# Stage 1 written out step by step, the real spectra of w first, GpSimd's fold of v without its wait for the selection

## The chip, the cores and the metric

The kernel runs on one core of one Trainium2 chip. The metric is the device time of one execution in microseconds (us). TensorE multiplies matrices into PSUM banks, VectorE and ScalarE work on SBUF and PSUM, GpSimd on SBUF, and SyncE only issues DMA transfers. Each engine runs its own instruction list in order; they wait for each other by semaphores.

## The reference

`x` and `ctx` are 8 x 512 x 2048. The first half of the reference is an autocorrelation attention, the second an expert layer with a dense base (2048 x 2048) on every row:

```
q = layernorm(x);  k = v = ctx                       # sequence length L = 512, per channel
corr = ifft(fft(q) * conj(fft(k))).real
w, idx = top_k(corr, 12);  w = softmax(w)
out = sum_i w_i * v[min(idx_i + pos, L - 1)]         # clamped shift
x = x + tanh(g_xattn) * out
x = x + tanh(g_ffn) * ffn(layernorm(x))              # base matmul, gates, 8 experts of rank 16
```

## The kernel before, in words

Stage 1 computes the attention for 8 sequences x 4 chunks of 512 channels: 32 steps (`STEPS`), a step being one chunk of one sequence. All spectra are matrix products with cosine and sine tables. Inputs are mirrored and folded into sums and differences of halves first, so that the tables are 128 x 128. Stage 2 (`tensor_dense` and the like) is not touched by the change.

For chunk i the work is:
- SyncE loads v, x and the chunk for the statistics (`load_v`, `load_x`, `load_stats`) and stores results (`store`).
- GpSimd folds v (`fold_v`, L871 and L872; `join_v`, L877 and L879), adds the products of q and k (`sum_qk`, L884), folds q (`fold_q`, L860 to L864) and adds the products of w and v (`sum_wv`, six times L897).
- TensorE: `v_spectra`, `q_spectra` (L414), `correlate` (L465), and for the chunk before `turn_w` (transposes, L427), `w_spectra` (L446 with the upper part of w, L452 with the lower), `out_tiles` (L482).
- VectorE: `q_times_k` (L680 to L688), `w_low` (L695), `w_times_v` (L708 to L719 with the spectra of the first half of w, L726 to L734 with the second), `largest` (L752 to L768), `select` (four L777, then the reciprocal L781). L777 keeps the weights of the twelve largest: it reads `corr` and `halves`, both in SBUF, and adds them up. Every fourth step it also computes the layer norm's scales for the next sequence (`variance`, `scales`), whose last operation signals `ln1_ready`.
- ScalarE: `copy_w` (L552), `normalise` (L529), `take_stats` (L586 to L593), `copy_odd` (L559), `copy_v`, `exponentials`, `keep_out` (L579), `scale_w` (L572).

The steps overlap: in step i the engines correlate chunk i, fold and transform v of chunk i + 1, and transform w of chunk i - 1. TensorE's order in step i is `turn_w(i-1)`, `w_spectra(i-1)`, `correlate(i)`, `v_spectra(i+1)`, `out_tiles(i-1, 1)`, `q_spectra(i+1)`, `out_tiles(i-1, 0)`. VectorE's is `q_times_k(i)`, `w_low(i-1)`, `w_times_v(i-1)`, `largest(i)`, `select(i)`. GpSimd's is `fold_v(i+1)`, `join_v(i+1)`, `sum_qk(i)`, `fold_q(i+1)`, `sum_wv(i-1)`. ScalarE's is `copy_w(i-1)`, `normalise(i+1)`, `take_stats(i+5)`, `copy_odd(i)`, `copy_v(i+1, False)`, `exponentials(i)`, `copy_v(i+1, True)`, `keep_out(i-1, 1)`, `scale_w(i)`, `keep_out(i-1, 0)`.

Eight PSUM banks are used in two groups of four, `mine` and `other`, which swap each step. `v_spectra` writes its imaginary parts (L398) into banks that `w_times_v` reads until L734.

Steps 2 to 25 are a hardware loop of six turns with four steps each (L265); the others are written out. SyncE's list is written out in full.

Two waits of GpSimd ahead of `fold_v` matter here: for `w_made`, which counts the L777 of the step before, and, in steps 3, 7, ... 27, for `ln1_ready`.

```
if least(i) >= 1 and most(i) + 1 < STEPS:
    pool.wait_ge(w_made, 4 * i)
    if phase == NCH - 1 and most(i) + NCH < STEPS:
        pool.wait_ge(ln1_ready, i // NCH + 2)
    fold_v(i + 1)
```

Of the kernel before, what the change touches and what calls it, by code (L numbers as in the profile page):

```python
# [111 lines left out]
def flamingo_kernel(nc, x, ctx_v, g_xattn, g_ffn, w_base, b_base, w_gate, w_thr, b_thr, a_w, b_w,  # L112
# [26 lines left out]
    with whole:  # L139
# [26 lines left out]
        with ExitStack() as s:  # L166
# [85 lines left out]

            LOOP, TURN = (2, STEPS - 6), NCH

            def least(i):
                return i if isinstance(i, int) else LOOP[0]

            def most(i):
                return i if isinstance(i, int) else LOOP[1] - 1
# [19 lines left out]
            def sync_attention(sp):  # L279
# [8 lines left out]
                def load_v(i):  # L288
                    if least(i) >= 1:
                        sp.wait_ge(v_symmed, 2 * i)  # L290
                    load_mirrored(vt, v_after, v_before, i, v_loaded)
# [12 lines left out]
                def load_x(i):  # L304
                    if least(i) >= 1:
# [14 lines left out]
                def load_stats(n):  # L320

                    if least(n) > NCH:
# [60 lines left out]
            def tensor_attention(pe):  # L383
                def v_spectra(n, at, four):

                    real, imag = pair(four, 0), pair(four, 1)
                    if least(n) >= 2:
# [7 lines left out]
                    if least(n) >= 2:  # L395
# [3 lines left out]
                    pe.matmul(imag[:, 1, :], v_tab[:, OI, :], v_sym[:, 3, :], start=True, stop=True).then_inc(v_made, 1)  # L399
                    pe.wait_ge(v_copied, 4 * n + 1)  # L400
# [1005 lines left out]
```

## Time and profile before

| what | us |
|---|---|
| median of 3 runs | 3023.3 (3022.74 to 3027.27) |
| profiled execution, its own time | 3029.54 |
| its span in the profile | 3027.7 |
| TensorE busy | 2836.9 |
| GpSimd busy | 1663.5 |
| VectorE busy | 1559.0 |
| ScalarE busy | 1081.3 |

The span runs from the first to the last instruction of the profiled execution. Busy time is the sum of the engine's instructions. Stage 1 fills about the first 1430 us of the span.

### The profile page before, as it was taken

The numbers are of one execution on the slowest core, as the hardware profiler recorded it, in microseconds if no ns is written. First come the engines' busy times: TensorE is split into PE (matmuls) and PEld (weight loads), VectorE is DVE, ScalarE is ACT, GpSimd is POOL, SyncE is SP. The second block draws the span as 40 slices with busy tenths as digits, with TensorE's granted clock in tenths as the row PEclk, the third lists the DMA queues.
The fourth block names the chain that finished last, engine by engine and source line by source line (L and its number), as shares of the span: only waits on it lengthen the run. The fifth ranks groups of instructions, "written<-read, shape, count | busy, mean of one in ns | idle before, by whom it ended". The sixth has DMA issues, their size and how long they took to land.

```text
span 3027.7 us, 37355 instructions
## 1 busy us (share of the span) xinstructions
PE 2836.9 (94%) x12932; PEld 1422.9 (47%) x12932; DVE 1559.0 (51%) x2646; ACT 1081.3 (36%) x1739; POOL 1663.5 (55%) x606
## 2 busy tenths in 40 slices
PE   4699999999999999997799999999999999999999
PEld 2345444444444444443544444444444444444444
DVE  3688989898898889998512122121221212112121
ACT  2556655556655565442422111121211212112120
POOL 3688888988888888884043332424334243342430
PEclk8899999999999999999999999999999999999999
DMA  5554545554555544344755544445444454454541
GB/s 150 111 132 121 128 115 131 130 128 118 126 124 133 128 120 111 93 125 127 277 167 160 160 152 158 147 159 159 152 153 152 156 161 154 152 152 152 160 132 42
DMA packets 276377, 424.72 MB, mean 140 GB/s; under 512 B 168047, under 2 KB 168623, under 8 KB 248885
## 3 DMA queue, kind: packets, MB, share of 16 engines
q1 hardware_dynamic: 257218, 288.98, 36.4%
q10 hardware_dynamic: 19068, 134.73, 13.0%
q8 instruction: 32, 0.52, 0.1%
q14 instruction: 59, 0.48, 0.1%
HBM read 256.79 MB, written 134.32 MB: 129 GB/s over the span
## 4 chain that ended last, share of the span: by engine, by line
PE 57%; DVE 19%; issue 9%; POOL 8%; DMA 3%; ACT 1%; SPq 1%; DVEq 0%; ACTq 0%; POOLq 0%
PE bank L1118 42%; PE bank L482 3%; DVE rows_mem L1316 2%; PE bank L446 2%; DVE top L759 1%; PE bank L414 1%; DVE corr_mem L777 1%; POOL spec_o L897 1%; DVE top L768 1%; DVE term L730 1%; POOL rows_mem L860 1%; POOL rows_mem L861 1%; DVE bank L731 1%; PE bank L1107 1%; PE bank L1108 1%
## 5 line engine op out<-in xcount | busy, mean ns | idle before, releaser
L1309 DVE TENSOR_TENSOR hwt_lo<-bank,hwt_hi 128x128 f16<-128x128 f32 x32 | 9.3, 292 | 1071.5 <-ACT hwt_hi L1199 1071.5
L1341 POOL TENSOR_TENSOR rows_mem<-norm,rows_mem 128x2048 f16<-128x2048 f32 x31 | 126.2, 4070 | 702.8 <-ACT rows_mem L1180 702.8
L1118 PE MATMUL bank<-w_hi,rows_mem 128*128 128x512 f16 x2048 | 489.3, 379 | 3.8 <-DVE rows_mem L1316 3.8
L1118 PE MATMUL bank<-w_hi,parts_mem 128*128 128x512 f16 x2048 | 489.4, 379 | 3.5 <-DVE rows_mem L1316 3.5
L1199 ACT ACTIVATE hwt_hi<-bank 128x128 f16<-128x128 f32 x32 | 8.9, 277 | 930.2 <-PE bank L1126 930.2
L1118 PEld LDWEIGHTS bank<-w_hi,rows_mem 128*128 128x128 f16 x2048 | 200.2, 98 | 251.7 <-DVE rows_mem L1316 13.7
L1118 PEld LDWEIGHTS bank<-w_hi,parts_mem 128*128 128x128 f16 x2048 | 200.4, 98 | 250.9 <-DVE rows_mem L1316 12.8
L897 POOL TENSOR_TENSOR spec_o<-spec_o,term 128x1024 f32<-128x1024 f32 x127 | 296.8, 2360 | 32.9 <-DVE term L713 30.0
L465 PE MATMUL bank<-table,prods 128*128 128x256 f32 x1024 | 236.3, 384 | 38.2 <-DVE spec_o L719 33.6
L1118 PE MATMUL bank<-w_lo,rows_mem 128*128 128x512 f16 x1024 | 262.8, 379 | 0.0
L1118 PE MATMUL bank<-w_lo,parts_mem 128*128 128x512 f16 x1024 | 262.8, 379 | 0.0
L482 PE MATMUL bank<-spec_o,table 128*128 128x512 f32 x512 | 251.1, 614 | 11.4 <-POOL spec_o L897 7.0
L446 PE MATMUL bank<-wt,table 128*128 128x512 f16 x1024 | 233.6, 379 | 7.3 <-DVE prods L688 7.0
L465 PEld LDWEIGHTS bank<-table,prods 128*128 128x128 f32 x1024 | 193.1, 191 | 79.6 <-DVE spec_o L719 46.0
L1347 POOL TENSOR_TENSOR norm<-norm,rows_mem 128x2048 f32<-128x2048 f32 x31 | 139.6, 4505 | 158.8 <-DMA rows_mem<-parts_behind 81.6
L1345 POOL TENSOR_TENSOR norm<-norm,rows_mem 128x2048 f32<-128x2048 f32 x31 | 139.6, 4502 | 121.4 <-DMA norm<-in_x_dram 121.4
L871 POOL TENSOR_TENSOR rows_mem<-rows_mem 128x1024 f32<-128x1024 f32 x32 | 75.8, 2368 | 232.7 <-DVE corr_mem L777 124.0
L1353 POOL TENSOR_TENSOR rows_mem<-rows_mem,b_rows 128x2048 f32<-128x2048 f32 x32 | 144.2, 4505 | 36.3 <-DMA rows_mem<-x_scratch 36.3
L1118 PEld LDWEIGHTS bank<-w_lo,parts_mem 128*128 128x128 f16 x1024 | 100.1, 98 | 119.1
L1118 PEld LDWEIGHTS bank<-w_lo,rows_mem 128*128 128x128 f16 x1024 | 100.2, 98 | 119.0
L446 PEld LDWEIGHTS bank<-wt,table 128*128 128x128 f16 x1024 | 96.7, 98 | 126.1 <-DVE prods L688 13.2
L482 PEld LDWEIGHTS bank<-spec_o,table 128*128 128x128 f32 x512 | 93.0, 192 | 118.8 <-issue 106.5
(199 smaller groups left out, 5178.8 us busy)
## 6 DMA issues: line engine op xcount, KB each, us to landing
parts_behind<-parts_mem SPq DMA_DIRECT2D x256, 128.0 KB
parts_ahead<-parts_mem SPq DMA_DIRECT2D x128, 256.0 KB
rows_mem<-x_scratch SPq DMA_DIRECT2D x32, 1024.0 KB, 4.8
rows_mem<-parts_behind ACTq DMA_DIRECT2D x32, 1024.0 KB, 6.1
out_dram<-rows_mem SPq DMA_DIRECT2D x32, 1024.0 KB, 3.9
norm<-in_x_dram ACTq DMA_DIRECT2D x31, 1024.0 KB, 5.6
x_scratch<-norm ACTq DMA_DIRECT2D x31, 1024.0 KB, 4.9
rows_mem<-parts_ahead ACTq DMA_DIRECT2D x30, 1024.0 KB, 5.9
```

The source lines that it names most:

```text
L414: mm = pe.matmul(pair(four, half)[:, row, :], v_tab[:, 2 * half + row, :], q_sym[:, 2 * half + row, :], start=True, stop=True)
L446: pe.matmul(pair(to, half)[:, row, :], w_tab[:, h, 2 * half + row, j, :], wt16[:, 0, 2 * y + j, :], start=(j == 0 and h == 0), stop=False)
L465: mm = pe.matmul(four[:, ct, row * HALF:(row + 1) * HALF], prod_a[:, slot, ct * 128:(ct + 1) * 128], p_tab[:, slot, :], start=(half == 0), ...
L482: mm = pe.matmul(to[:, part, :], o_tab[:, slot, :], spec_o[:, h, slot, :], start=(row == 0), stop=(part == 1 and row == 1))
L871: pool.tensor_tensor(v_sym[:, 0:2, :], vt[:, 0:2, :], vt[:, 2:4, :], ALU.add).then_inc(v_symmed, 1)
L897: pool.tensor_tensor(to, to, buffer, sign).then_inc(term_added, 1)
L1118: mm = pe.matmul(dense[o][:, :], nt(par, part)[:, k, :], w[:, k, o * 512:(o + 1) * 512], start=(k == 0 and n == 0), stop=False)
L1316: dve.scalar_tensor_tensor(out=row[:, cols], in0=dense[o][:, :], scalar=out_gate[:, :], in1=row[:, cols], op0=ALU.mult, op1=ALU.add).then_ ...
L1341: pool.tensor_tensor(norm_lo, norm[:, :], norm_hi, ALU.subtract).then_inc(norm_lo_made, 1)
L1345: pool.tensor_tensor(norm[:, :], norm[:, :], addend, ALU.add).then_inc(formed, 1)
L1347: pool.tensor_tensor(norm[:, :], norm[:, :], addend, (ALU.subtract, ALU.add)[par]).then_inc(formed, 1)
L1353: pool.tensor_tensor(row, row, bias[:, :], ALU.add).then_inc(bias_added, 1)
```

## The change

`least`, `most` and the loop are gone: all 33 turns of `step` are written out on every engine. `w_spectra` makes a pair of real spectra complete (upper and lower part of w) before it begins the imaginary ones. `keep_out` copies the cosine bank and the sine bank apart, and `turn_w` waits for each by itself. GpSimd no longer waits for `w_made` ahead of `fold_v`; its wait for `ln1_ready` stays. In the first steps the square root comes ahead of `copy_v`, the turn of the scales lies inside `v_spectra(0)`, `load_stats(4)` ahead of `load_x(1)`, `take_stats(5)` behind `scale_w(0)`, `join_v(1)` behind `sum_qk(0)`, `fold_v(1)` waits for VectorE's `fold_q(0)`, and the loads of the experts' B are spread over steps 4 to 11. Lines that only lose `least` and `most` are left out:

```diff
             def steps(eng, step):
-                for i in range(LOOP[0]):
-                    step(i, i % 2, i % NCH)
-                with eng.Fori(0, (LOOP[1] - LOOP[0]) // TURN) as m:
-                    for u in range(LOOP[0], LOOP[0] + TURN):
-                        step(TURN * m + u, u % 2, u % NCH)
-                for i in range(LOOP[1], STEPS + 1):
+                for i in range(STEPS + 1):
                     step(i, i % 2, i % NCH)
...
                 load_v(1)
                 load_v_last(1)
+                load_stats(NCH)
                 load_x(1)
                 sp.dma_start(table16[:, :], tables16).then_inc(table16_loaded, 16)
-                load_stats(NCH)
-                load_stats(NCH + 1)
                 b_view = b_rows[:, :].rearrange("p (n e r) -> p n e r", e=E, r=R)
-                for e in range(E):
-                    sp.dma_start(b_view[:, :, e, :], b_w[e].rearrange("(n p) r -> p n r", p=128)).then_inc(b_loaded, 16)
 
                 def step(i, par, phase):
                     if i + 2 < STEPS:
                         load_v(i + 2)
                         load_v_last(i + 2)
+                    if i == 0:
+                        load_stats(NCH + 1)
+                        load_x(2)
                     if i + NCH + 2 < STEPS:
                         load_stats(i + NCH + 2)
-                    if i + 2 < STEPS:
+                    if 1 <= i and i + 2 < STEPS:
                         load_x(i + 2)
+                    if NCH <= i < NCH + E:
+                        e = i - NCH
+                        sp.dma_start(b_view[:, :, e, :], b_w[e].rearrange("(n p) r -> p n r", p=128)).then_inc(b_loaded, 16)
...
                     pe.matmul(imag[:, 1, :], v_tab[:, OI, :], v_sym[:, 3, :], start=True, stop=True).then_inc(v_made, 1)
+                    if n == 0:
+                        turn_scales()
...
                 def turn_w(c, four):
-                    for y in range(2):
-                        if least(c) >= 1:
-                            pe.wait_ge(out_kept, 2 * (c - 1) + y + 1)
...
+                    if c >= 1:
+                        pe.wait_ge(out_kept, 2 * c - 1)
+                    for ct in range(CT):
+                        pe.wait_ge(w_scaled, 4 * c + ct + 1)
+                        for j in range(2):
+                            mm = pe.transpose(pair(four, 0)[:, j, ct * 128:(ct + 1) * 128],
+                                              corr[:, ct, j * 128:(j + 1) * 128], ident[:, :])
+                    mm.then_inc(w_turned, 1)
+                    for j in range(2):
+                        if c >= 1 and j == 0:
+                            pe.wait_ge(cos_kept, c)
+                        elif c >= 1:
+                            pe.wait_ge(out_kept, 2 * c)
...
                 def w_spectra(c, mine, other):
...
                                         pe.matmul(pair(to, half)[:, row, :], w_tab[:, h, 2 * half + row, j, :],
                                                   wt16[:, 0, 2 * y + j, :], start=(j == 0 and h == 0), stop=False)
-                        pe.wait_ge(w_lo_made, 2 * c + y + 1)
-                        for half in range(2):
+                            if half == 0:
+                                pe.wait_ge(w_lo_made, 2 * c + y + 1)
                             for row in range(2):
                                 for j in range(2):
...
                 def keep_out(c, four, h):
...
+                    if h == 1:
+                        act.wait_ge(out_made, 2 * c + 1)
+                        act.activation(kept[:, 1, :, :], pair(four, 0), ACT.Copy, scale=gates[:, 0:1]).then_inc(out_kept, 1)
+                    else:
+                        act.wait_ge(cos_made, c + 1)
+                        act.activation(kept[:, 0, 0, :], pair(four, 1)[:, 0, :], ACT.Copy, scale=gates[:, 0:1])\
+                           .then_inc(cos_kept, 1)
+                        act.wait_ge(out_made, 2 * c + 2)
+                        act.activation(kept[:, 0, 1, :], pair(four, 1)[:, 1, :], ACT.Copy, scale=gates[:, 0:1])\
+                           .then_inc(out_kept, 1)
...
+                deviation(0)
                 copy_v(0, 0, X(0), False)
-                deviation(0)
                 normalise(0)
...
-                    if most(i) + NCH + 1 < STEPS:
+                    if 1 <= i and i + NCH + 1 < STEPS:
                         take_stats(i + NCH + 1, (phase + 1) % NCH)
...
                         keep_out(i - 1, mine, 0)
+                    else:
+                        take_stats(NCH + 1, 1)
...
                 fold_v(0)
                 join_v(0)
+
+                pool.wait_ge(q_folded, 4)
                 fold_v(1)
...
-                    if least(i) >= 1 and most(i) + 1 < STEPS:
-                        pool.wait_ge(w_made, 4 * i)
-                        if phase == NCH - 1 and most(i) + NCH < STEPS:
+                    if i >= 1 and i + 1 < STEPS:
+                        if phase == NCH - 1 and i + NCH < STEPS:
                             pool.wait_ge(ln1_ready, i // NCH + 2)
                         fold_v(i + 1)
-                    if most(i) + 1 < STEPS:
+                    if 1 <= i and i + 1 < STEPS:
                         join_v(i + 1)
-                    if most(i) < STEPS:
+                    if i < STEPS:
                         sum_qk(i)
-                    if most(i) + 1 < STEPS:
+                    if i == 0:
+                        join_v(1)
+                    if i + 1 < STEPS:
                         fold_q(pool, i + 1)
```

`turn_scales` is the former code between `v_spectra(0)` and `q_spectra(0)`, L493 to L498. `out_tiles` signals `cos_made` once its cosine bank is done.

## Rows read from the trace of the kernel before

**Rows 1.** The page, busy us (share of the span) and instructions of each engine.

```profile
PE 2836.9 (94%) x12932; PEld 1422.9 (47%) x12932; DVE 1559.0 (51%) x2646; ACT 1081.3 (36%) x1739; POOL 1663.5 (55%) x606
```

**Rows 2.** Timeline, VectorE, one inner step: start us, us, instruction, idle before and releaser.

```profile
778.97 0.18 DVE L781 RECIPROCAL w_inv<-w_sum 128x4 f32<-128x4 f32 x1
...
785.43 2.44 DVE L695 SCALAR_TENSOR_TENSOR wt<-bank,wt 128x1024 f16<-128x1024 f32 x2 [0.15 <-ACT wt L552]
790.01 1.23 DVE L708 TENSOR_TENSOR spec_o<-bank,spec_v 128x1024 f32<-128x1024 f32 x1 [2.13 <-PE bank L452]
...
805.28 1.23 DVE L734 TENSOR_TENSOR prods<-bank,prods 128x1024 f32<-128x1024 f32 x1
...
816.79 0.75 DVE L777 SCALAR_TENSOR_TENSOR corr_mem<-corr_mem,top,halves 128x512 f32<-128x512 f32 x1 [0.22 <-DVE top L768]
...
819.60 0.18 DVE L781 RECIPROCAL w_inv<-w_sum 128x4 f32<-128x4 f32 x1
823.13 1.22 DVE L680 TENSOR_TENSOR prods<-bank,spec_v 128x1024 f32<-128x1024 f32 x1 [3.34 <-issue]
```

**Rows 3.** Timeline, TensorE, the same step.

```profile
783.10 1.04 PE L427 MATMUL bank<-ident,corr_mem 128*128 128x128 f32 x8
...
785.40 3.62 PE L446 MATMUL bank<-wt,table 128*128 128x512 f16 x16
...
800.48 3.72 PE L465 MATMUL bank<-table,prods 128*128 128x256 f32 x16 [1.11 <-DVE spec_o L719]
...
806.64 1.12 PE L398 MATMUL bank<-rows_mem,table 128*128 128x512 f32 x2 [0.19 <-DVE prods L734]
```

**Rows 4.** Timeline, GpSimd: a step with the wait for `ln1_ready`, then the step above.

```profile
717.86 6.99 POOL L897 TENSOR_TENSOR spec_o<-spec_o,term 128x1024 f32<-128x1024 f32 x3
...
779.16 2.37 POOL L871 TENSOR_TENSOR rows_mem<-rows_mem 128x1024 f32<-128x1024 f32 x1 [6.57 <-DVE corr_mem L777]
...
791.00 2.38 POOL L860 TENSOR_TENSOR rows_mem<-rows_mem 128x1024 f32<-128x1024 f32 x1
...
800.42 7.01 POOL L897 TENSOR_TENSOR spec_o<-spec_o,term 128x1024 f32<-128x1024 f32 x3
...
812.14 2.37 POOL L897 TENSOR_TENSOR spec_o<-spec_o,prods 128x1024 f32<-128x1024 f32 x1
```

**Rows 5.** Waits of the whole span: who waited for whom, us, times, longest us.

```profile
POOL rows_mem L871 <- DVE corr_mem L777: 124.0, 22, 6.6
...
DVE term L730 <- POOL spec_o L897: 15.4, 7, 2.2
```

**Rows 6.** Timeline, ScalarE, the start of the same step.

```profile
779.18 2.56 ACT L572 ACTIVATE corr_mem<-corr_mem,w_inv 128x512 f32<-128x512 f32 x4 [1.73 <-DVE w_inv L781]
783.30 1.11 ACT L579 ACTIVATE parts_mem<-bank,gates 128x1024 f32<-128x1024 f32 x1 [1.56 <-PE bank L482]
...
786.52 2.92 ACT L529 ACTIVATE rows_mem<-rows_mem,ln_bias,ln_scale 128x512 f32<-128x512 f32 x4
```

**Rows 7.** Timeline, VectorE's `fold_q(0)` beside GpSimd's `join_v(1)`.

```profile
45.62 3.20 POOL L877 TENSOR_TENSOR v_odd<-rows_mem 128x1024 f32<-128x1024 f32 x1
...
46.55 3.35 DVE L861 TENSOR_TENSOR rows_mem<-rows_mem 128x1024 f32<-128x1024 f32 x1
...
53.11 1.21 DVE L864 TENSOR_TENSOR parts_mem<-rows_mem 128x1024 f32<-128x1024 f32 x1
```

**Rows 8.** Timeline, the first step on three engines, and the last step's L781.

```profile
38.87 0.18 DVE L99 RECIPROCAL ln_rows<-std 128x4 f32<-128x4 f32 x1 [8.42 <-ACT std L599]
...
64.50 8.83 PE L465 MATMUL bank<-table,prods 128*128 128x256 f32 x32 [4.58 <-POOL prods L884]
...
89.32 1.00 ACT L559 ACTIVATE halves<-bank 128x1024 f32<-128x1024 f32 x1
...
103.35 0.18 DVE L781 RECIPROCAL w_inv<-w_sum 128x4 f32<-128x4 f32 x1
...
1401.42 0.18 DVE L781 RECIPROCAL w_inv<-w_sum 128x4 f32<-128x4 f32 x1
```

More of the change, by code:

```diff
@@ L383, in tensor_attention, with turn_scales @@
             def tensor_attention(pe):
+                def turn_scales():
+                    pe.wait_ge(ident_loaded, 16)
+                    pe.wait_ge(order_made, 2)
+                    pe.wait_ge(ln1_step, 6)
+                    for n in range(2):
+                        mm = pe.matmul(bank[7][:, 4 * n:4 * n + 4], order[:, n, :], ln1_rows[:, :, 1 - n::2],
+                                       start=True, stop=True)
+                    mm.then_inc(ln1_turned, 1)
                 def v_spectra(n, at, four):
                     real, imag = pair(four, 0), pair(four, 1)
-                    if least(n) >= 2:
+                    if n >= 2:
                         pe.wait_ge(term_made, 12 * (n - 2) + 10)
@@ L436, in w_spectra @@
                         for half in range(2):
-                            if y == 0 and most(c) + 1 < STEPS:
+                            if y == 0 and c + 1 < STEPS:
                                 pe.wait_ge(q_used, 2 * (c + 1) + half + 1)
@@ L459, in correlate @@
                     for ct in range(CT):
-                        if ct % 2 == 0 and least(i) >= 1:
+                        if ct % 2 == 0 and i >= 1:
                             pe.wait_ge(term_made, 12 * (i - 1) + (4 if ct == 0 else 8))
@@ L470, in out_tiles @@
                 def out_tiles(c, at, four, h):
-                    if most(c) + 1 < STEPS:
+                    if c + 1 < STEPS:
                         pe.wait_ge(corr_split, 2 * (c + 2))
-                    if h == 0 and most(c) == STEPS - 1:
+                    if h == 0 and c == STEPS - 1:
                         pe.wait_ge(late_added, 3)
@@ L484, in out_tiles @@
                         if part == 0:
[L485 removed]
+                            mm = pe.matmul(to[:, 0, :], last_tab[:, 3, :], v_last[:, at, :], start=False, stop=True)
+                            if h == 0:
+                                mm.then_inc(cos_made, 1)
                     mm.then_inc(out_made, 1)
@@ L490, in tensor_attention @@
                 v_spectra(0, 0, X(0))
-                pe.wait_ge(ident_loaded, 16)
-                pe.wait_ge(order_made, 2)
-                pe.wait_ge(ln1_step, 6)
-                for n in range(2):
-                    mm = pe.matmul(bank[7][:, 4 * n:4 * n + 4], order[:, n, :], ln1_rows[:, :, 1 - n::2], start=True, stop=True)
-                mm.then_inc(ln1_turned, 1)
                 q_spectra(0, X(0))
@@ L535, in copy_v @@
                     first = 4 * n + 2 * whole_v
-                    if not whole_v and least(n) >= 2:
+                    if not whole_v and n >= 2:
                         act.wait_ge(term_made, 12 * (n - 1))
@@ L722, in w_times_v @@
                         dve.wait_ge(wspec_made, 4 * c + 3)
-                        if most(c) + 1 < STEPS:
+                        if c + 1 < STEPS:
                             dve.wait_ge(q_used, 2 * (c + 2))
@@ L821, in step @@
                     mine, other = X(par), X(1 - par)
-                    more = most(i) + NCH + 1 < STEPS and phase == NCH - 2
-                    if most(i) < STEPS:
+                    more = i + NCH + 1 < STEPS and phase == NCH - 2
+                    if i < STEPS:
                         q_times_k(i, par, mine)
-                    if most(i) == STEPS:
+                    if i == STEPS:
                         moments(dve, 0)
-                    if least(i) >= 1:
+                    if i >= 1:
                         w_low(i - 1, other)
-                    if most(i) == STEPS:
+                    if i == STEPS:
                         scale_rows(dve, 0)
-                    if least(i) >= 1:
+                    if i >= 1:
                         w_times_v(i - 1, 1 - par, mine, other, 0)
-                    if least(i) >= 1:
+                    if i >= 1:
                         w_times_v(i - 1, 1 - par, mine, other, 1)
-                    if most(i) == STEPS:
+                    if i == STEPS:
                         late_sums(i - 1)
                         weights_lo(dve, 0, 2)
-                    if most(i) < STEPS:
+                    if i < STEPS:
                         largest(i, mine)
@@ L891, in sum_wv @@
                             (o0r, ALU.add, late[0], 9, 1), (o0r, ALU.add, t[2], 11, 4), (o0i, ALU.add, late[1], 12, 2)]
-                    for to, sign, buffer, made, own in todo if most(c) + 1 < STEPS else todo[0:3]:
+                    for to, sign, buffer, made, own in todo if c + 1 < STEPS else todo[0:3]:
                         pool.wait_ge(term_made, 12 * c + made)
```

89 lines of the change are left out of this document (39 added, 50 removed).

## The prediction

> **What bounds the kernel now.** I read the page first: TensorE is busy in 94% of the span, VectorE and GpSimd in half [rows 1]. The change lies in stage 1 alone (its 32 steps, about 1400 us), so I then read one inner step in order of time, engine by engine, and from it the cycles that can set a step's length. A step is counted from one end of `select` (the reciprocal L781) to the next: 40.63 us here [rows 2].
>
> Three cycles compete.
> - VectorE alone, if it never waits: L781 ends at 779.15; five products and both `w_low` are done at 787.87, 8.7 later of which 0.3 is waiting, so 8.4; L708 to the end of L734 is 16.5 (790.01 to 806.51); to the first L777 10.3; L777 to the end of L781 3.0. Sum 38.2 us. It waited 2.13 at L708 for L452 [rows 2].
> - TensorE and VectorE in turn: the end of L734 frees banks for L398 (806.64), from there TensorE works to the next `turn_w` (783.10 + 40.63 = 823.73), 17.1; `turn_w` to L708 6.9; L708 to L734's end 16.5; 0.1 between. Sum 40.6: this one sets the step now [rows 2, 3].
> - TensorE alone: 40.6 less its gaps of 1.1 and 0.2, at most 39.3 [rows 3].
>
> GpSimd waits at the start of each step for the end of `select` (6.57 us here), then has fifteen operations of 2.36 us [rows 4]. It holds up L730 in 7 steps, those in which it also waits for `ln1_ready`: 15.4 us in all [rows 5].
>
> **The change, part by part.**
>
> *Real spectra first.* L708 needed 16 matmuls of L446 and 4 of L452; now it needs 8 and 4. Sixteen of L446 take 3.62 with the last one's tail, so eight are 1.7 us [rows 3]. The second cycle falls to 38.9, so that TensorE alone (39.3) and VectorE (38.2) are next. The split of `keep_out` and its second wait on TensorE move some 0.3 us and sit beside TensorE work; I take nothing, with 0.2 us a step as bound both ways (6 us in all).
>
> *No loop.* Once in four steps VectorE stands 3.34 us at the turn with no releaser [rows 2]. TensorE has queued work then (it was at `out_tiles`), so of this only what exceeds VectorE's 2.4 us of slack comes through, about 1 us in six turns. Below, VectorE becomes the bound and the 3.3 us are gained in full. The Trainium skill (Advanced Engine Details and Errata, Control Flow Timing) gives a compare-and-branch about 108 ns; by that six turns would cost 0.6 us, and the row, at 3.34 us for one, disagrees.
>
> *The removed wait.* GpSimd starts the fold at 779.16, once L777 is done: four operations of `fold_v` and `join_v`. Its last sum of the step ends at 814.51, but the first L777 begins at 816.79 [rows 2, 4]. Today no L777 meets a busy GpSimd. Without the wait, the fold starts as soon as the sums end and runs straight through the select. L777 reads two SBUF tensors (`corr` and `halves`). The only place where VectorE did that beside a busy GpSimd is `fold_q(0)`: L861 took 3.35 us, L864, with GpSimd done, 1.21; GpSimd's L877 took 3.20 in place of 2.36 [rows 4, 7]. The sums fit strict alternation: VectorE waits out one GpSimd operation (2.3), works 1.15, and GpSimd waits that long. L777 is another operation than L861, so its price lies between 0 and, if all four meet an operation, 4 x 2.36 = 9.4 us a select. I take the alternation, by the nearest row.
> The Trainium skill (SBUF — State Buffer, Who interferes with whom) says that a VectorE instruction with two SBUF inputs contends with GpSimd instructions that read SBUF, under an exclusive lock. By it L777 must block as L861 does and the sum is the one that follows; by a reading of the rows that confines it to the plain add, the wait would be nothing.
>
> How far GpSimd has come at the select, counted from the end R of the last one: ScalarE's `scale_w` 2.6, then the `keep_out` and both `copy_w` 3.3 (783.30 to 786.52), `normalise` 2.9: R + 8.8 [rows 6]. Only then can `fold_q` start (four operations, 9.4), then six sums (800.42 to 814.51, 14.1): GpSimd is free at R + 32.3 [rows 4]. So removing the wait hardly moves the end of GpSimd's chain: `normalise` holds `fold_q`. VectorE reaches L777 at R + 8.4 + 16.5 + 10.3 = R + 35.2. By then the first operation of the fold is over and the second has 2 x 2.36 - 2.9 = 1.8 us to go. The first L777 waits for that, the second and third 2.3 each behind the two of `join_v`; the fourth is free since `sum_qk` waits for VectorE itself. In all 6.4 us. The step becomes 38.2 + 6.4 = 44.6, VectorE bound, and the spectra's 1.7 us are worth nothing in it.
>
> *Kinds of step.* (a) Steps 3, 7, ... 27, where `ln1_ready` still holds the fold: L897 started at 717.86, L730 follows it by 2.4, L777 is another 3.7 + 10.3 later, at 734.3. By [rows 4] the fifteen operations began 21.3 before 717.86, at 696.6, and the seven tiny instructions ahead of them (0.2 each, as L99 [rows 8]) at R = 695.0; with 3.0 of L777 and L781 that step takes 42.3, as now. GpSimd ends at 717.86 + 14.1 = 731.9, 2.4 before L777, so 7.0 are added: 49.3. (b) Steps 2, 6, ... 26: the fold behind their select still waits, nothing collides; 38.2 plus seven tiny instructions, 39.5. (c) Steps 30 and 31: no fold; 39. (d) The other 14 from step 4 on, 44.6. (e) Step 1: `take_stats(5)` now stands ahead of `copy_w(0)`; ScalarE's `w_hi` is 4.6 us later than in (d), 3.2 at L708 and some more at L730 and the lock, 49.
> Sum for steps 1 to 31: 7 x 49.3 + 7 x 39.5 + 2 x 39 + 14 x 44.6 + 49 = 1373. Before it was 1401.42 - 103.35 = 1298.1 [rows 8]. Added: 75 us.
>
> *First steps.* Newton's start waited 8.42 for the square root; moved ahead, about 4 come through, since `normalise(0)` now stands behind `copy_v`. GpSimd's fold waits for `fold_q(0)`, which loses its alternation: L861 to L864 took 6.56 for two operations, now 2.3, and L860 gains 1: 5. So the first products come 9 earlier. `copy_odd(0)` ran at 89.32 since it stood behind two `take_stats` and the loads they wait for. Now only `correlate(0)` is ahead (64.50 to 73.3, now 9 earlier): 24 to 25 earlier [rows 7, 8]. The first select meets the fold of step 1 (+6): R(0) is 18 earlier, 85. The fold of step 1 loses its old cover, the late load of v; the loads of b move into steps 4 to 11, ahead of `store(i - 1)` and the next step's loads on SyncE; no fold in the steady steps is idle for a load (22 times the releaser is L777, else `ln1_ready`) [rows 5], so I take 0, and without that cover each would cost its issue, eight in all. `load_stats(5)` and `load_stats(6)` wait on SyncE for `take_stats`, with v(3) and x(3) queued behind them, which GpSimd and ScalarE want a step later. Bounds for this part: 10 to 30 us gained.
>
> Total: 75 - 18 = +57 to the profiled execution's 3029.5 (span 3027.7), so 3086; that execution is 6 us above the median, hence **3080 us** against 3023.3.
>
> **Rivals.**
> 1. *No lock for L777* (other side): it is a fused operation with an accumulator and no row shows it beside GpSimd. Then (a) stays 42.3, (b) 40.3 (39.3 and the tiny ones' share), the rest 39.4 by TensorE: 7 x 42.3 + 7 x 40.3 + 17 x 39.4 = 1248, 50 less; the start gains 24: 2950. For it: only the row of L861 speaks of contention. Against: same two SBUF inputs. It decides at the point where a select loses 3.2 us: 23 collisions (steps 0 to 29 without the seven of (b)) x 3.2 = 74, the gain without a lock.
> 2. *VectorE waits once*, for the running operation, and its four L777 then pass together: 1.7 (2.4 in (a)): (a) 44.7, (b) 40.3, the rest 39.9: 1273, 25 less, start 22: 2976. Against: GpSimd's L877 got in between L860 and L861, which were back to back [rows 7].
> 3. *Every L777 collides* (fold found later, or joins stretched): 9.4 in each of 23: 3080 + 23 x 3 = 3149.
> 4. *Nothing comes of it*: a lock of about 3.2 us a select: 3023.
>
> **Numbers.** Forecast 0.72 (its own range 3045 to 3110: 1 us in the meeting point over 23 selects, and 10 of the start), rival 1 0.12, rival 2 0.09, rival 3 0.04, rival 4 0.03. Leaving out rival 1 and rival 3, with edges of the forecast, the range is 2970 to 3110. Within 0.2% (6 us, about what a measurement here can tell): 0.03. Faster 0.21, slower 0.76.
>
> **What would show it.** L777's mean grows from 0.75 to about 1.9 us (23 x 6.4 over 128, and 0.75), with 1.7 to 2.4 us more on three of four; L872, L877 and L879 grow by 0.7; steps 44.6 apart, 49.3 in (a); TensorE idle some 3 us before `turn_w`, its clock lower. `copy_odd(0)` near 65 and L781 of step 0 near 85. Wrong if L777 stays 0.75 (rival 1), if only the first of four grows (rival 2), or if `fold_v` ends before L777 begins, because `normalise` let `fold_q` start earlier than R + 8.8.

## The result and the profile after

The changed kernel takes 3063.26 us in the median of four runs (3062.31 to 3063.63), the kernel before 3025.28 in four (3022.74 to 3028.23): a ratio of 1.0125, with a 95% interval of 1.0107 to 1.0142. The forecast was 3080, slower, with 0.76 on that side, its range 2970 to 3110. The profiled execution took 3062.31 us, its span is 3060.5, 32.8 longer than before, and TensorE's mean granted clock is 0.978 in place of 0.984.

The span falls into three parts at the ends of `select`. R(i) stands for the end of the reciprocal (L781, now L794) of step i.

| part, us | before | after | difference | forecast |
|---|---|---|---|---|
| start to R(0) | 103.5 | 87.3 | -16.2 | -18 |
| R(0) to R(31) | 1298.1 | 1349.9 | +51.8 | +75 |
| R(31) to the end | 1626.1 | 1623.3 | -2.8 | 0 |

The first and the last L794 of the changed kernel (timeline of VectorE: start us, us, instruction); those of before are in [rows 8].

```profile
87.13 0.18 DVE L794 RECIPROCAL w_inv<-w_sum 128x4 f32<-128x4 f32 x1
...
1437.08 0.18 DVE L794 RECIPROCAL w_inv<-w_sum 128x4 f32<-128x4 f32 x1
```

The page's first part, busy us, share of the span and instructions of each engine (before: [rows 1]), then the rows of L790 and, from before, of L777, which is the same instruction: busy us and mean ns.

```profile
PE 2871.9 (94%) x12932; PEld 1436.4 (47%) x12932; DVE 1693.0 (55%) x2646; ACT 1082.8 (35%) x1771; POOL 1683.4 (55%) x606
...
L790 DVE SCALAR_TENSOR_TENSOR corr_mem<-corr_mem,top,halves 128x512 f32<-128x512 f32 x128 | 230.1, 1850 | 0.9
```

```profile
L777 DVE SCALAR_TENSOR_TENSOR corr_mem<-corr_mem,top,halves 128x512 f32<-128x512 f32 x128 | 88.7, 748 | 4.5 <-DVE top L768 4.0
```

VectorE has the same 2646 instructions and is busy 134 us longer. One line accounts for it: L790 went from a mean of 0.75 us to 1.85, in sum 141 us more, or 6.1 for each of the 23 selects that meet the fold. The profile does not call this waiting. It is booked as busy time of an instruction that got slower, and in the table of waits VectorE looks better than before: its wait ahead of the first product with the weights' spectra, L708 there and L721 here, fell from 47.6 us to 5.7. The row of before (us, times, longest):

```profile
DVE spec_o L708 <- PE bank L452: 47.6, 32, 2.1
```

The timeline of VectorE (start us, us, instruction, idle before and its releaser) in an inner step, which answers to [rows 2]:

```profile
783.08 2.64 DVE L790 SCALAR_TENSOR_TENSOR corr_mem<-corr_mem,top,halves 128x512 f32<-128x512 f32 x1
...
785.65 2.83 DVE L790 SCALAR_TENSOR_TENSOR corr_mem<-corr_mem,top,halves 128x512 f32<-128x512 f32 x1
...
788.41 2.82 DVE L790 SCALAR_TENSOR_TENSOR corr_mem<-corr_mem,top,halves 128x512 f32<-128x512 f32 x1
...
791.16 0.74 DVE L790 SCALAR_TENSOR_TENSOR corr_mem<-corr_mem,top,halves 128x512 f32<-128x512 f32 x1
...
791.94 0.18 DVE L794 RECIPROCAL w_inv<-w_sum 128x4 f32<-128x4 f32 x1
...
800.92 1.22 DVE L721 TENSOR_TENSOR spec_o<-bank,spec_v 128x1024 f32<-128x1024 f32 x1 [0.58 <-PE bank L461]
802.07 1.21 DVE L722 TENSOR_TENSOR term<-bank,spec_v 128x1024 f32<-128x1024 f32 x1
...
827.29 2.49 DVE L790 SCALAR_TENSOR_TENSOR corr_mem<-corr_mem,top,halves 128x512 f32<-128x512 f32 x1
...
836.00 0.18 DVE L794 RECIPROCAL w_inv<-w_sum 128x4 f32<-128x4 f32 x1
```

GpSimd in the same stretch, which answers to [rows 4]:

```profile
780.49 2.37 POOL L884 TENSOR_TENSOR rows_mem<-rows_mem 128x1024 f32<-128x1024 f32 x1
782.80 2.36 POOL L885 TENSOR_TENSOR rows_mem<-rows_mem 128x1024 f32<-128x1024 f32 x1
785.25 2.68 POOL L890 TENSOR_TENSOR v_odd<-rows_mem 128x1024 f32<-128x1024 f32 x1
788.01 2.67 POOL L892 TENSOR_TENSOR rows_mem<-rows_mem 128x1024 f32<-128x1024 f32 x1
...
801.04 2.37 POOL L873 TENSOR_TENSOR rows_mem<-rows_mem 128x1024 f32<-128x1024 f32 x1 [2.94 <-ACT rows_mem L532]
```

The two engines take turns. The first L790 is issued 0.3 us after L885 began and ends at 785.7, half a microsecond after L885 does. The second ends half a microsecond after L890, the third half a microsecond after L892. GpSimd has nothing more to do then, since L897 needs VectorE's next products, and the fourth takes 0.74. So the select takes 9.0 us instead of 3.0, and the step 44.1 (791.94 to 836.00) instead of 40.6. The rows also show what GpSimd gained by starting early: nothing. `fold_q` (L873) waits 2.94 us for `normalise` (L532) and starts at 801.04, 8.9 after R.

This is one of two patterns. In 9 of the 23 selects the first three L790 pay and the fourth is free, as above. In 13 the first begins just before L885 does, takes 0.76 and holds L885 up, and the other three pay; so it is in this step (timelines of VectorE and GpSimd):

```profile
1001.93 0.76 DVE L790 SCALAR_TENSOR_TENSOR corr_mem<-corr_mem,top,halves 128x512 f32<-128x512 f32 x1
...
1002.62 2.82 DVE L790 SCALAR_TENSOR_TENSOR corr_mem<-corr_mem,top,halves 128x512 f32<-128x512 f32 x1
```

```profile
1002.05 2.85 POOL L885 TENSOR_TENSOR rows_mem<-rows_mem 128x1024 f32<-128x1024 f32 x1
```

The price hardly differs: 5.9 to 6.1 us a select in seven of the first kind (5.2 and 5.6 in steps 1 and 0), 6.2 in the second. In step 3 all four pay, 7.3.

The waits of the whole span (us, times, longest), with GpSimd's row for the wait that was removed gone and two in its place (before: [rows 5]):

```profile
POOL prods L897 <- DVE prods L697: 109.8, 24, 5.1
...
POOL rows_mem L873 <- ACT rows_mem L532: 73.4, 24, 6.9
```

GpSimd stood 124 us for L777 before and 29 at these two places; at them it now stands 183. TensorE, in its timeline, stands 2.3 us ahead of `turn_w` in this step, and 1.1 to 2.8 in the others from step 2 on that follow a select which met the fold:

```profile
793.02 0.96 PE L427 MATMUL bank<-ident,corr_mem 128*128 128x128 f32 x4 [2.32 <-ACT corr_mem L575]
```

And the page's sum over the chain that ended last (before: PE 57%, DVE 19%) says which engine lengthens the steps:

```profile
PE 50%; DVE 30%; POOL 7%; issue 7%; DMA 3%; ACT 2%; SPq 1%; DVEq 0%; ACTq 0%; POOLq 0%
```

### The profile page after: what moved, and what is told of

It reads as the page before. It is cut to its first block, busy times and chain, and to the rows that moved or that the text cites. A ratio compares the mean times of both kernels' runs of the same rounds, so it can differ in the third digit from the quotient of the medians.

```text
span 3060.5 us, 36056 instructions
## 1 busy us (share of the span) xinstructions
PE 2871.9 (94%) x12932; PEld 1436.4 (47%) x12932; DVE 1693.0 (55%) x2646; ACT 1082.8 (35%) x1771; POOL 1683.4 (55%) x606
## 4 chain that ended last, share of the span: by engine, by line
PE 50%; DVE 30%; POOL 7%; issue 7%; DMA 3%; ACT 2%; SPq 1%; DVEq 0%; ACTq 0%; POOLq 0%
PE bank L1134 41%; DVE corr_mem L790 6%; DVE top L772 3%; DVE top L781 2%; DVE rows_mem L1332 2%; DVE corr_mem L765 1%; DVE term L743 1%; DVE corr_mem L766 1%; ACT corr_mem L575 1%; DVE bank L744 1%; DVE prods L776 1%; PE bank L455 1%; POOL spec_o L910 1%; PE bank L1123 1%; PE bank L1124 1%
## 5 line engine op out<-in xcount | busy, mean ns | idle before, releaser
L455 PE MATMUL bank<-wt,table 128*128 128x512 f16 x1024 | 252.9, 392 | 7.9 <-ACT wt L555 7.9
L474 PE MATMUL bank<-table,prods 128*128 128x256 f32 x1024 | 227.9, 381 | 9.1 <-DMA table<-in_tables_dram 9.1
L790 DVE SCALAR_TENSOR_TENSOR corr_mem<-corr_mem,top,halves 128x512 f32<-128x512 f32 x128 | 230.1, 1850 | 0.9
```

Of the source, the lines that this page charges most:

```text
L455: pe.matmul(pair(to, half)[:, row, :], w_tab[:, h, 2 * half + row, j, :], wt16[:, 0, 2 * y + j, :], start=(j == 0 and h == 0), stop=False)
L474: mm = pe.matmul(four[:, ct, row * HALF:(row + 1) * HALF], prod_a[:, slot, ct * 128:(ct + 1) * 128], p_tab[:, slot, :], start=(half == 0), ...
L790: dve.scalar_tensor_tensor(out=corr[:, ct, :], in0=corr[:, ct, :], scalar=top[:, ct, TOPK - 1:TOPK], in1=halves[:, ct, :], op0=ALU.is_ge, ...
```

## The experiments

Ten more kernels were run, each beside runs of the kernel before on the same chip (medians 3025 to 3028 us), to which the ratios refer. "Changed" is the kernel after.

| kernel | median us | ratio to before (95%) | mean L790, us | R(0) | R(0) to R(31) |
|---|---|---|---|---|---|
| before | 3025.28 | | 0.75 | 103.5 | 1298.1 |
| changed | 3063.26 | 1.0125 (1.0107 to 1.0142) | 1.85 | 87.3 | 1349.9 |
| e1, changed, wait put back | 2975.27 | 0.9825 (0.9809 to 0.9842) | 0.75 | 83.0 | 1270.1 |
| e2, before, only the wait removed | 3123.63 | 1.0311 (1.0292 to 1.0330) | 1.66 | 102.6 | 1393.2 |
| e3, changed, select with one SBUF tensor | 2957.62 | 0.9765 (0.9749 to 0.9782) | 0.74 | 83.5 | 1252.4 |
| e6, changed, old order of spectra | 3082.94 | 1.0183 (1.0166 to 1.0200) | 1.69 | 88.9 | 1369.0 |
| e4, changed, half of `fold_v` ahead of the wait | 2933.49 | 0.9690 (0.9674 to 0.9706) | 0.75 | 82.8 | 1228.0 |
| e5, changed, whole `fold_v` ahead of the wait | 2952.77 | 0.9752 (0.9735 to 0.9768) | 1.03 | 84.0 | 1244.9 |
| e7, changed, start of GpSimd unheld | 3064.18 | 1.0119 (1.0098 to 1.0140) | 1.85 | 88.6 | 1350.6 |
| e8, e5 with `take_stats(5)` later | 2954.18 | 0.9759 (0.9742 to 0.9776) | 1.04 | 84.1 | 1246.1 |
| e9, e4 with the old order of spectra | 2968.4 | 0.9805 (0.9788 to 0.9821) | 0.75 | 82.8 | 1262.2 |
| e10, e4 with `table16` loaded earlier | 2927.73 | 0.9673 (0.9657 to 0.9690) | 0.75 | 76.3 | 1228.1 |

**e1: the wait for the select back in the changed kernel.**

```
     def step(i, par, phase):
         ...
         if i >= 1 and i + 1 < STEPS:
+            pool.wait_ge(w_made, 4 * i)
             if phase == NCH - 1 and i + NCH < STEPS:
                 pool.wait_ge(ln1_ready, i // NCH + 2)
             fold_v(i + 1)
```

> The changed kernel with one thing undone: GpSimd waits for w_made again ahead of fold_v. Lock theory: the four L777 of a select (L790 in the changed kernel) fall back from 1.85 us to 0.75 each, about 6 us a select in 23 selects. But the step does not fall to TensorE's 39.3: GpSimd then starts its fold at R, reaches the end of its first sum at R + 21.3 + 2.4 and frees L730 (now L743) at R + 23.7, and 3.7 + 10.3 + 3.0 us later the step ends, so 40.7 us, as long as before. Total about 2985 us (2975 to 2995), the gain over the kernel before coming mostly from the first steps (some 22 us). Rival (the loss lies in the written-out list or in TensorE's clock, not in the select): L790 may fall, the time stays near 3060.

2975.27 us, 88 less than the changed kernel and 50 less than the one before. One line decides the sign of the whole change. L790 is back to 0.75 (row of its group, then of the waits: us, times, longest):

```profile
L790 DVE SCALAR_TENSOR_TENSOR corr_mem<-corr_mem,top,halves 128x512 f32<-128x512 f32 x128 | 88.7, 748 | 0.9
```

```profile
DVE term L743 <- POOL spec_o L910: 47.1, 24, 2.9
```

The second row is what the expectation had worked out: with the wait back GpSimd's first sum comes too late for L743, and the steps of the common kind stay at 40.4 us (40.7 expected). It is late 24 times. In the kernel before it was late 8 times over the whole span, as this row shows; the row in [rows 5], 7 times and 15.4 us, covers 150 to 1400 us and not the whole span.

```profile
DVE term L730 <- POOL spec_o L897: 23.0, 8, 7.6
```

VectorE reaches L743 earlier than it reached L730, since its spectra are ready earlier. So the wait is dear for GpSimd and its absence dearer for VectorE, which is the lead to e4.

**e2: the kernel before, with the wait removed and nothing else.**

```
                     if least(i) >= 1 and most(i) + 1 < STEPS:
-                        pool.wait_ge(w_made, 4 * i)
                         if phase == NCH - 1 and most(i) + NCH < STEPS:
```

> The kernel before with only the wait for w_made taken out, all else as it was. Lock theory: the same locks as in the changed kernel, without what the other edits give back: +52 us in steps 1 to 31 as measured there, +3.3 us at each of six loop turns since VectorE is now the bound, +1 us a step at L708 since the 16 + 4 matmuls end later than w_low: about 3115 us (3095 to 3130). Rival (the other edits cost the time): 3023, or a little less since GpSimd folds earlier.

3123.63 us, in the expected range of 3095 to 3130. With e1 this makes a square of four kernels: without the rest of the change the removal costs 96 us (3123.6 against the 3027.6 of its own chip), with it 88; the rest gains 50 where the wait stands (3025 to 2975) and 60 where it does not (3124 to 3063). Removing the wait is the whole loss, and all else together is a gain.

**e3: the select reads one SBUF tensor.** L790 compares `corr` with the threshold and sums, but leaves out the product with the exponentials (`halves`), so the weights are ones and zeros. The waits are those of the changed kernel.

```
-    dve.scalar_tensor_tensor(out=corr[:, ct, :], in0=corr[:, ct, :], scalar=top[:, ct, TOPK - 1:TOPK],
-                             in1=halves[:, ct, :], op0=ALU.is_ge, op1=ALU.mult,
-                             accum_out=w_sum[:, ct:ct + 1]).then_inc(w_made, 1)
+    dve.tensor_scalar(corr[:, ct, :], corr[:, ct, :], top[:, ct, TOPK - 1:TOPK], None, ALU.is_ge,
+                      ALU.add, accum_out=w_sum[:, ct:ct + 1]).then_inc(w_made, 1)
```

> The changed kernel with the select's four operations reading one SBUF tensor: a tensor_scalar keeps corr >= threshold and adds it up; the product with the exponentials (halves) is left out, so the kept weights are all equal. Everything else, and GpSimd's order, is as in the changed kernel. Lock theory (two SBUF inputs against a GpSimd operation that reads SBUF): no lock, each of the four at about 0.7 us, steps of about 39.3 us by TensorE, total 2950 us (2940 to 2965). Rival (any VectorE operation on SBUF at that place is slowed by GpSimd's running fold, or the delay is the semaphore order): each stays near 1.8 us and the time near 3060.

2957.62 us, in the expected range of 2940 to 2965. In an inner step its four L790 run from 731.47 to 734.2, 0.74 each, while GpSimd does the two operations of `fold_v` at 2.35 and 2.36 (timeline of each engine; the fold's lines are one lower here):

```profile
731.47 0.74 DVE L790 TENSOR_SCALAR_CACHE_REDUCE corr_mem<-corr_mem,top 128x512 f32<-128x512 f32 x1
...
733.48 0.74 DVE L790 TENSOR_SCALAR_CACHE_REDUCE corr_mem<-corr_mem,top 128x512 f32<-128x512 f32 x1
```

```profile
729.32 2.35 POOL L883 TENSOR_TENSOR rows_mem<-rows_mem 128x1024 f32<-128x1024 f32 x1
731.64 2.36 POOL L884 TENSOR_TENSOR rows_mem<-rows_mem 128x1024 f32<-128x1024 f32 x1
```

Same elements, same accumulator, same neighbours in time, one SBUF input fewer: no lock. That a second SBUF input is what makes VectorE wait for GpSimd is what the Trainium skill says (SBUF — State Buffer, Who interferes with whom), and the pair 1.85 against 0.74 us agrees. e3 changes the operation along with the number of inputs, so by itself it doesn't tell the two apart. The plain `TENSOR_TENSOR` does: with both inputs in SBUF it took 3.35 us beside GpSimd [rows 7], with one of them in PSUM it took 1.21 (L722 at 802.07, in the middle of L873, above).

**e6: the old order of the spectra in the changed kernel.** The forecast took the reordering to be worth nothing where the lock binds.

```
-                            if half == 0:
-                                pe.wait_ge(w_lo_made, 2 * c + y + 1)
+                        pe.wait_ge(w_lo_made, 2 * c + y + 1)
+                        for half in range(2):
                             for row in range(2):
                                 for j in range(2):
```

(The matmuls with `w_lo` stand again in a loop of their own, behind those with `w_hi`.)

> The changed kernel with the old order in w_spectra (all of the upper part of w, then all of the lower). By the prediction the reordering is worth nothing where VectorE is the bound: 3063. By a second working out: w_hi is there at R + 4.8, sixteen and four matmuls then take 4.3 us and L708 (L721) starts at R + 9.4 in place of R + 8.4, so 1 us a step in some 22 steps that are not held by GpSimd: 3085.

3082.94 us, 20 more than the changed kernel, as the second working out of the expectation had it (3085). VectorE's wait at L721, the old L708, over the span (us, times, longest), here and in the changed kernel:

```profile
DVE spec_o L721 <- PE bank L461: 54.5, 32, 3.7
```

```profile
DVE spec_o L721 <- PE bank L461: 5.7, 10, 2.1
```

The 49 us of waiting come back, and 20 reach the end. Of the rest, 20 us are offset at the select, which is asked for later and meets less of the fold (L790's mean 1.69, its sum 20 us less). The wait in an inner step of e6 (VectorE's timeline):

```profile
1022.83 0.18 DVE L794 RECIPROCAL w_inv<-w_sum 128x4 f32<-128x4 f32 x1
...
1033.30 1.22 DVE L721 TENSOR_TENSOR spec_o<-bank,spec_v 128x1024 f32<-128x1024 f32 x1 [2.07 <-PE bank L461]
```

From R to L721 it is 10.3 us here and 8.8 in the changed kernel (792.12 to 800.92). "Worth nothing" was wrong.

**e4: one operation of `fold_v` ahead of the wait.** GpSimd ends its sums 2.3 us before the select begins [rows 2, 4], and one operation takes 2.36.

```
-                def fold_v(n):
+                def fold_v(n, whole=True):
...
                     pool.tensor_tensor(v_sym[:, 0:2, :], vt[:, 0:2, :], vt[:, 2:4, :], ALU.add).then_inc(v_symmed, 1)
+                    if not whole:
+                        return
+                    fold_v_rest(n)
+
+                def fold_v_rest(n):
                     pool.tensor_tensor(v_sym[:, 2:4, :], vt[:, 0:2, :], vt[:, 2:4, :], ALU.subtract).then_inc(v_symmed, 1)
...
                     if i >= 1 and i + 1 < STEPS:
+                        fold_v(i + 1, False)
+                        pool.wait_ge(w_made, 4 * i)
                         if phase == NCH - 1 and i + NCH < STEPS:
                             pool.wait_ge(ln1_ready, i // NCH + 2)
-                        fold_v(i + 1)
+                        fold_v_rest(i + 1)
                     if 1 <= i and i + 1 < STEPS:
                         join_v(i + 1)
```

> The changed kernel with fold_v cut in two: its first operation goes ahead of the wait, then GpSimd waits for w_made (and ln1_ready) as before, then come the second operation and join_v. Lock theory with its clockwork: the first operation runs in the 3 us between GpSimd's last sum and the first L790, so no lock (L790 at 0.75 us), and GpSimd's chain behind the wait is 2.35 us shorter: its steps of 40.4 in e1_wait_back fall to TensorE's 39.0, the ln1_ready steps from 41.9 to about 39.8. Steps 1 to 31: about 1222 us against 1270; total 2930 us (2922 to 2940). Rival (the wait as such costs little, GpSimd is not what holds e1_wait_back): 2975, no change.

2933.49 us, 0.9690 of before (0.9674 to 0.9706), and within 4 us of the expectation. GpSimd's timeline (in this kernel L890 is the second operation of `fold_v`):

```profile
714.84 2.38 POOL L884 TENSOR_TENSOR rows_mem<-rows_mem 128x1024 f32<-128x1024 f32 x1
719.88 2.38 POOL L890 TENSOR_TENSOR rows_mem<-rows_mem 128x1024 f32<-128x1024 f32 x1 [2.66 <-DVE corr_mem L790]
```

```profile
716.99 0.79 DVE L790 SCALAR_TENSOR_TENSOR corr_mem<-corr_mem,top,halves 128x512 f32<-128x512 f32 x1
...
717.71 0.74 DVE L790 SCALAR_TENSOR_TENSOR corr_mem<-corr_mem,top,halves 128x512 f32<-128x512 f32 x1
```

GpSimd fills the gap before the select, stands still for its 2.66 us, and goes on. The first L790 loses 0.04 us, the others nothing: steps 1 to 31 are 39.6 us on average, near the 39.3 that the forecast had worked out for TensorE alone.

```profile
PE 2812.8 (96%) x12932; PEld 1419.5 (48%) x12932; DVE 1555.4 (53%) x2646; ACT 1088.7 (37%) x1771; POOL 1663.9 (57%) x606
```

**e9: e4 with the old order of the spectra** (the edits of e4 and e6 together).

> e4_first_half with the old order in w_spectra. Theory of the three cycles: with neither the lock nor GpSimd in the way, the cycle of TensorE and VectorE (40.6 with the old order, 38.9 with the new) comes out: steps of 40.4 in place of 38.9 to 39.6 where GpSimd doesn't hold them, so the reordering is worth 1 to 1.6 us in some 24 steps: 2933 + 25 to 40 = about 2965. Rival (the reordering only helps VectorE's wait, hidden by other work): within 6 us of 2933.

2968.4 us, 35 more than e4, where the same edit cost 20 in the changed kernel. A shorter wait of one engine is worth most where nothing else binds it.

**e5: both operations of `fold_v` ahead of the wait.**

```
                     if i >= 1 and i + 1 < STEPS:
+                        fold_v(i + 1)
+                        pool.wait_ge(w_made, 4 * i)
                         if phase == NCH - 1 and i + NCH < STEPS:
                             pool.wait_ge(ln1_ready, i // NCH + 2)
-                        fold_v(i + 1)
```

> As e4_first_half, but both operations of fold_v ahead of the wait, join_v behind it. Lock theory: the second operation is still running when the first L790 starts, for 0.5 to 2 us, and then GpSimd stands at the wait, so only the first of four grows, to about 2 us; VectorE has 1 us of slack a step against TensorE. Steps 39.0 to 40, total 2920 to 2945, within 10 us of e4_first_half. If any L790 but the first grows, the alternation is not what sets them.

2952.77 us, 19 more than e4; within 10 was expected. One step in the timelines of VectorE and GpSimd:

```profile
726.11 0.76 DVE L790 SCALAR_TENSOR_TENSOR corr_mem<-corr_mem,top,halves 128x512 f32<-128x512 f32 x1
...
726.80 2.83 DVE L790 SCALAR_TENSOR_TENSOR corr_mem<-corr_mem,top,halves 128x512 f32<-128x512 f32 x1
...
729.56 0.74 DVE L790 SCALAR_TENSOR_TENSOR corr_mem<-corr_mem,top,halves 128x512 f32<-128x512 f32 x1
```

```profile
723.95 2.37 POOL L884 TENSOR_TENSOR rows_mem<-rows_mem 128x1024 f32<-128x1024 f32 x1
726.27 2.80 POOL L885 TENSOR_TENSOR rows_mem<-rows_mem 128x1024 f32<-128x1024 f32 x1
731.06 2.38 POOL L890 TENSOR_TENSOR v_odd<-rows_mem 128x1024 f32<-128x1024 f32 x1 [1.98 <-DVE corr_mem L790]
```

Every select that meets the fold pays once. In 16 of the 23 it is the first L790 that grows, by 0.9 to 1.8 us, since it meets L885 part of the way through. In the other 7, the steps 4, 8, ... 28, it is the second, as above, by 2.1: the first began within the last 0.2 us of L884 and held L885 up (2.80). The expectation had said that growth of any but the first would speak against the alternation. That went too far: the same taking of turns gives it, once the first L790 gets in ahead of L885.

This is a dose curve: none met 2933 (e4), one 2953 (e5), three 3063 (changed). L790's sum over the span is 88.9, 125.1 and 230.1 us. From e4 to e5 it grows by 36, of which 19 reach the time, and from e5 to the changed kernel by 105, where the time grows by 110.

**e7: GpSimd's start unheld.** The changed kernel without the new wait for `fold_q(0)` at the start:

```
                 join_v(0)
-                pool.wait_ge(q_folded, 4)
                 fold_v(1)
```

> The changed kernel without GpSimd's wait for fold_q(0) ahead of fold_v(1). By the prediction this wait saves 5 us. By the trace of the changed kernel correlate(0) stands 9 us at the table's load, so the lock at fold_q(0) returns (its operations at 2.3 to 3.4 us) but costs nothing: L794 of step 0 within 1 us of 87.3, time 3063.

3064.18 us, ratio 1.0119 (1.0098 to 1.0140), R(0) 88.6: no difference that the times tell. The timelines of VectorE and GpSimd:

```profile
42.28 1.22 DVE L877 TENSOR_TENSOR parts_mem<-rows_mem 128x1024 f32<-128x1024 f32 x1
```

```profile
42.72 2.98 POOL L884 TENSOR_TENSOR rows_mem<-rows_mem 128x1024 f32<-128x1024 f32 x1 [8.92 <-DMA rows_mem<-in_ctx_dram]
```

GpSimd waits for the load of v(1), which lands at 42.7, and `fold_q(0)` is at its last operation by then. So only that one overlaps, and here GpSimd is the one held (L884 takes 2.98 us against 2.34 in the changed kernel). The lock at `fold_q(0)`, which the expectation had return, does not: VectorE's four operations take 1.22 or 1.23 each. What parted the two is above all the earlier square root (VectorE's L99, with which it begins the scales for `normalise(0)`, is at 33.7 in the changed kernel, 38.87 before [rows 8]), and a little the load, since before `fold_v(1)` could begin at 40.90.

**e8: `take_stats(5)` behind `copy_w(0)`,** in e5:

```
                     if i >= 1:
                         copy_w(i - 1, other)
+                    if i == 1:
+                        take_stats(NCH + 1, 1)
...
                         keep_out(i - 1, mine, 0)
-                    else:
-                        take_stats(NCH + 1, 1)
```

> e5_both_halves with take_stats(5) moved behind copy_w(0), so that ScalarE's copies of w in step 1 come 5.4 us earlier. Step 1 should fall by 2 to 3 us (L721's wait of 2.05 and what GpSimd loses), the load of statistics 6 and what queues behind it on SyncE starts some 5 us later without a wait coming of it. Time 1 to 3 us below e5_both_halves. Rival: the time in step 1 is held by GpSimd and nothing moves.

2954.18 against 2952.77: nothing, where 1 to 3 us less were expected. Step 1 does not get shorter (44.9 us, 44.0 in e5). The rival in the expectation holds: VectorE's waits at L708 and L721 (3.06 and 2.38 us in e5) are gone, and it stands at L743 for GpSimd instead (timeline of VectorE).

```profile
109.40 1.23 DVE L743 TENSOR_TENSOR term<-bank,spec_v 128x1024 f32<-128x1024 f32 x1 [4.45 <-POOL spec_o L910]
```

GpSimd's `fold_q(2)` waits in both for `normalise(2)` (5.79 us in e5, 6.42 here), and `take_stats(5)` is ahead of that in either place.

**e10: the table of the correlation earlier,** in e4. TensorE stood 9.05 us ahead of `correlate(0)` in the changed kernel (timeline):

```profile
58.66 8.78 PE L474 MATMUL bank<-table,prods 128*128 128x256 f32 x32 [9.05 <-DMA table<-in_tables_dram]
```

```
                 load_v_last(1)
+                sp.dma_start(table16[:, :], tables16).then_inc(table16_loaded, 16)
                 load_stats(NCH)
                 load_x(1)
-                sp.dma_start(table16[:, :], tables16).then_inc(table16_loaded, 16)
```

> e4_first_half with the load of table16 issued ahead of load_stats(4) and load_x(1). In the changed kernel correlate(0) stands 9 us at this table; its other inputs are there 5 us before it starts. The first select ends 4 to 5 us earlier (L794 at about 78) and the time falls to about 2929; rival: x(1) or the statistics come later by as much and hold ScalarE, no change.

2927.73 us (2929 expected), 5.8 less than e4, R(0) at 76.3 instead of 82.8, and now GpSimd is what TensorE waits for:

```profile
53.18 7.11 PE L474 MATMUL bank<-table,prods 128*128 128x256 f32 x24 [4.63 <-POOL prods L902]
```

It is the fastest of all: 0.9673 of the kernel before (0.9657 to 0.9690).

## Why the prediction was right, and where its terms were off

The mechanism stood as forecast: the removed wait gives GpSimd nothing (`fold_q` at R + 8.9, forecast R + 8.8; free at R + 32.5, forecast R + 32.3), the select is asked for at R + 35.2 as worked out, and from there its reads alternate with three GpSimd operations. Rivals 1 and 2 fall by L790's times in the changed kernel, rival 3 because three of the four pay in 22 of 23 selects, rival 4 by the time. The signs came too: L790's mean is 1.85 (1.9 forecast), TensorE stands ahead of `turn_w` (1.1 to 2.8 us, 3 forecast) and its clock is lower (0.978 against 0.984). e2 and e1 show that the removed wait is the loss; e3, with the plain operation of one and of two SBUF inputs, shows that the second SBUF input is its means.

The size was 57 us in the forecast; the spans show 32.8 and the medians 38.0. Of the 24 us between 57 and 32.8, the steps make 23 and the tail 3, and the start takes 2 back; so the total did not come right by errors that cancel, it came out too high by a row of small ones. Term by term:

- *Steps 1 to 31, 1373 forecast, 1349.9 measured.* (a) 7 x 49.3 = 345 against 337.8; (b) 276.5 against 271.6; (c) 78 against 76.6; (d) 14 x 44.6 = 624 against 616.0, 44.0 on average; (e) 49 against 47.9. Two causes. The lock cost 6.1 us a select, not 6.4 and 7.0: an L790 that follows another took 2.83, so 2.08 more than alone, where 2.3 was taken, and with the first L790 in ahead of L885 the other three pay, 6.2 in all. That is so in six steps of (a), while step 3 pays 7.3, and in seven of the 14 of (d), where the forecast had the first pay and the fourth free; since the price is nearly the same either way, the total doesn't show it. And VectorE alone needs 37.9 us a step (step 30), not 38.2.
- *The start, 18 forecast, 16.2 measured.* The first products came 10.8 us earlier (L693 at 47.47, L680 at 58.29 before) where 9 was forecast, but `correlate(0)` only 5.8 (58.66 against 64.50 [rows 8]), held by the load of `table16`, which the forecast did not look at; `copy_odd(0)` ran at 67.5, near the 65 forecast. The step "GpSimd's fold waits for `fold_q(0)`, which loses its alternation" had the right effect and the wrong cause: the alternation is gone without that wait too (e7).
- *The tail* is 2.8 us shorter, which was not forecast. It is 1626 us in the two kernels without the rest of the change (before and e2) and 1621 to 1625 in the other ten, so it belongs to that rest and not to the wait; the cause is open.
- *"The spectra's 1.7 us are worth nothing"* failed: they are worth 20 us in the changed kernel (e6) and 35 where the lock is gone (e9). The forecast laid the wait at L708 wholly to the cycle through L734 and `out_tiles`, which the lock gives slack. But there is a second way to L708: from R through `scale_w`, `turn_w`, `copy_w` and the spectra. It starts when the select ends, so the lock cannot cover it, and in the old order it takes 10.3 us against the 8.4 that VectorE itself needs (e6). The total was not touched, as the forecast costed the changed order.
- *"No loop":* the 3.34 us that VectorE stood at a turn are gone with the loop. No run here takes the unrolling alone, so its share of the 50 to 60 us is open. A bound comes from e2 and e6, both without the wait and with the old spectra: their steps 1 to 31 take 1393.2 and 1369.0 us, so the loop, the split of `keep_out` and the moved loads are worth 24 us there together.
- *GpSimd's share of the lock:* L890 and L892 grew to 2.68 and 2.67, by 0.3 each, not 0.7. L885 did not grow where the first L790 waited for it, and grew to 2.8 or 2.9 where the first got in ahead of it, seven times in (d).

## What to carry to other kernels

Before you take a wait away, ask whom it keeps apart. This one looked like a needless order between two engines without shared data, and it kept GpSimd quiet while VectorE read two SBUF tensors; its loss, 88 to 96 us, was larger than all that the rest of the change gained. The better edit does not remove such a wait but fills the gap before it, with as much of the other engine's work as ends before the sensitive instructions begin: the wait with one operation ahead of it is 130 us faster than no wait, 42 of them by the operation (e1 to e4), and a second operation lost 19 again. And when an instruction's mean grows without any change to it, look at what the other engine was doing in the same microseconds, because the waits list will not show it.

## What the runs showed of the hardware

- The alternation is operation by operation: of four VectorE instructions of 0.75 us in a row, three took 2.64, 2.83 and 2.82 us beside three GpSimd operations of 2.36, of which the two that began behind a waiting instruction took 2.68 and 2.67. Each of the three pays anew; they do not pass together once the first has waited.
- 2.83 is less than 2.36 + 0.75 = 3.11, so the wait leaves out 0.3 us of the reported times of the two; and a VectorE instruction can begin while the last 0.2 us of a GpSimd operation are still being reported (726.11 against 723.95 + 2.37 = 726.32) and take no longer; the GpSimd operation behind it then took 2.80 in place of 2.36.
- The fused select with accumulator is held as the plain sum at the start was [rows 7]; the compare with accumulator and one SBUF tensor is not, 0.74 us beside a running GpSimd (e3), nor is the plain operation with one input in PSUM, 1.21 us (L722 at 802.07 within L873, 801.04 to 803.41).
